# Router logits of a mixture-of-experts layer: the turned tokens as stationary operand, the router's 8 columns streaming

## The reference

```python
xf = x.reshape(-1, d)
gate_base = xf @ Wg.T
up_base = xf @ Wu.T
base_out = jax.nn.silu(gate_base) * up_base @ Wd.T
router_logits = xf @ Wr.T            # Wr is 8 x 256
probs = jax.nn.softmax(router_logits.astype(jnp.float32), axis=-1)
topw, topi = jax.lax.top_k(probs, K) # K = 2 of E = 8
...
def expert_step(acc, params):
    g_lora = xf @ Ag_e.T @ Bg_e.T * SCALING
    u_lora = xf @ Au_e.T @ Bu_e.T * SCALING
    h = jax.nn.silu(gate_base + g_lora) * (up_base + u_lora)
    d_delta = h @ Ad_e.T @ Bd_e.T * SCALING
    return (acc + d_delta * we[:, None], None)
```

## Time and profile before

| | |
|---|---|
| runs | 847.05, 847.84, 850.38 us, median 847.84 |
| the profiled execution's own time | 848.89 us |
| its span, first to last instruction | 847.2 us |
| TensorE busy | 737.8 us, 87% of the span, 4038 matmuls |
| VectorE, ScalarE, GpSimd busy | 524.9, 376.5 and 147.1 us |
| mean granted TensorE clock | 0.937 of full speed |

### The profile page before, as it was taken

One profiled execution on the slowest core, in us unless ns is written; L12 is line 12 of the kernel. 1 busy time (PEld: TensorE's weight loads), 2 busy tenths in 40 slices (PEclk: granted clock), 3 DMA queues, 4 the chain that ended last, 5 costly groups with the idle time before them and its releaser, 6 DMA issues. The chain is left out here.

```text
span 847.2 us, 10572 instructions
## 1 busy us (share of the span) xinstructions
PE 737.8 (87%) x4038; PEld 612.6 (72%) x4038; DVE 524.9 (62%) x927; ACT 376.5 (44%) x780; POOL 147.1 (17%) x115
## 2 busy tenths in 40 slices
PE   2798978775999999999999999999487999999956
PEld 1577767664787777887688777887265887878846
DVE  5545554654577545755475645755447888979883
ACT  4765545514465432544344433344255355254421
POOL 5065354331000001000010000000020223203110
PEclk9979999865999999999999999999689999999978
DMA  4075333100000000000000000040000000000000
GB/s 161 0 231 170 102 66 107 55 1 0 1 1 1 1 2 0 1 1 1 1 1 1 1 0 1 3 197 2 0 1 0 1 26 1 1 26 1 26 0 26
DMA packets 21282, 25.75 MB, mean 30 GB/s; under 512 B 976, under 2 KB 19408, under 8 KB 20464
## 3 DMA queue, kind: packets, MB, share of 16 engines
q1 hardware_dynamic: 20576, 23.76, 8.7%
q10 hardware_dynamic: 656, 1.31, 0.4%
HBM read 22.91 MB, written 2.16 MB: 30 GB/s over the span
## 5 line engine op out<-in xcount | busy, mean ns | idle before, releaser
L1014 DVE TENSOR_TENSOR h_raw<-h_s,bank 128x512 f32<-128x512 f32 x104 | 71.4, 687 | 148.3 <-ACT h_s L1004 129.6
L1004 ACT ACTIVATE h_s<-bank 128x512 f32<-128x512 f32 x104 | 62.1, 597 | 185.3 <-PE bank L91 185.3
L1019 DVE TENSOR_TENSOR h_ring_lo<-h_raw,h_ring_hi 128x512 fp32r<-128x512 f32 x104 | 76.9, 739 | 0.1
L1008 ACT ACTIVATE h_ring_hi<-h_raw 128x512 fp32r<-128x512 f32 x104 | 64.7, 622 | 0.2 <-DVE h_raw L1014 0.2
L90 PE MATMUL bank<-fused_lo,h_ring_hi 128*128 128x256 f32 (+1 forms) x224 | 62.8, 280 | 0.0
L89 PE MATMUL bank<-l_xT_hi,l_wgu 128*128 128x512 f32 x128 | 52.5, 410 | 8.2 <-DVE l_h L1899 5.9
L89 PE MATMUL bank<-f_xT_hi,ffn_hi 128*128 128x512 f32 (+2 forms) x120 | 47.8, 399 | 7.6 <-DVE f_xT_lo L1421 7.1
L1368 POOL TENSOR_TENSOR late_rstd<-f_vv,minus_half 128x4 f32<-128x4 f32 x4 | 4.0, 1009 | 289.1 <-DVE f_vv L1512 289.1
L89 PE MATMUL bank<-f_yT_hi,mlp_hi 128*128 128x512 f32 x128 | 52.4, 409 | 1.6 <-issue 1.6
L91 PE MATMUL bank<-l_xT_hi,l_lo 128*128 128x512 f32 x128 | 50.8, 397 | 0.0
L90 PE MATMUL bank<-l_xT_lo,l_wgu 128*128 128x512 f32 x128 | 50.8, 397 | 0.0
(11 more groups left out here) (303 smaller groups left out, 2112.4 us busy)
## 6 DMA issues: line engine op xcount, KB each, us to landing
m_W<-m_scratch SPq DMA_DIRECT2D x16, 512.0 KB, 5.9
fused_raw<-in_fused SPq DMA_DIRECT2D x1, 3584.0 KB, 15.9
res<-in_x SPq DMA_DIRECT2D x4, 512.0 KB, 6.1
fused_raw<-in_fused SPq DMA_DIRECT2D x2, 1024.0 KB, 8.3
l_raw<-in_layer SPq DMA_DIRECT2D x1, 2048.0 KB, 10.0
out_x<-res SPq DMA_DIRECT2D x16, 128.0 KB, 1.9
l_raw<-in_layer SPq DMA_DIRECT2D x1, 1280.0 KB, 12.4
fused_raw<-in_fused SPq DMA_DIRECT2D x1, 1120.0 KB, 5.1
```

The lines of the kernel that those rows point to most:

```text
L1004: self.nc.scalar.activation(self.s[u % 2][r, :], gate[r, :], ACT.Silu).then_inc(self.silu.sem, 1)
L1008: self.nc.scalar.activation(self.unit(i, u)[0], self.product(i, u), ACT.Copy).then_inc(self.hi.sem, 1)
L1014: self.nc.vector.tensor_tensor(out=self.product(i, u), in0=self.s[u % 2][r, :], in1=up[r, :], op=ALU.mult).then_inc(self.hidden.sem, 1)
L1019: self.nc.vector.tensor_tensor(out=lo, in0=self.product(i, u), in1=f32(hi), op=ALU.subtract).then_inc(self.lo.sem, 1)
```

## The change

The logits are made the other way round. For each chunk of 128 tokens the turned tokens are the stationary operand (128 x 128) and the router's 8 real columns stream, so the result has its tokens in the partitions at once. VectorE reads that result directly; the copy on ScalarE and the four turns on TensorE go away, and with them the tile `f_lg` and two semaphores.

```diff
@@ router_and_ranks
-                for k in range(KD):
-                    last = product(nc, turn_bank[0][0:EW, :], cut(wr, a, k), cut(xT, a, k), k == 0, k == KD - 1)
+                for c in range(C):
+                    for k in range(KD):
+                        last = product(nc, turn_bank[0][:, c * E:(c + 1) * E], cut(xT, a, k, chunk(c)), cut(wr, a, k, slice(0, E)), c == 0 and k == 0, k == KD - 1)
                 last.then_inc(lg_ready.sem, 1)
                 ranks(i, 0)
...
-            def turn_router(i):
-                pe.wait_ge(lg_copied.sem, lg_copied.at(i, 1))
-                for c in range(C):
-                    last = nc.tensor.transpose(turn_bank[0][:, c * EW:(c + 1) * EW], lg[:, chunk(c)], ident[0:EW, 0:EW])
-                last.then_inc(lgT.sem, 1)
...
-                    elif u == 4:
-                        turn_router(i)
...
-            def copy_router(i):
-                act.wait_ge(lg_ready.sem, lg_ready.at(i, 1))
-                nc.scalar.activation(lg[:, :], turn_bank[0][0:EW, :], ACT.Copy).then_inc(lg_copied.sem, 1)
...
-                        copy_router(i)
                         high_ranks(i, 0)
...
-            lgv = turn_bank[0][:, 0:C * EW].rearrange("p (c e) -> p c e", e=EW)[:, :, 0:E]
+            lgv = turn_bank[0][:, 0:C * E].rearrange("p (c e) -> p c e", e=E)
...
-                dve.wait_ge(lgT.sem, lgT.at(i, 1))
+                dve.wait_ge(lg_ready.sem, lg_ready.at(i, 1))
```

More of the change, by code:

```diff
@@ L1081, in fused_phase @@
     xs, ys = over("f_xs", [P, C, D]), over("f_ys", [P, C, D])
-    lg = Map(nc, spread_at + 4 * C * D)("f_lg", [EW, S])
     op0 = [m.pair("f_op0", [P, S])]
@@ L1104, in fused_phase @@
     yT_t, yT_hi, yT_lo, xs_ready, xT_t, xT_hi, xT_lo = (sg("f_" + n, 2) for n in ("yTt", "yThi", "yTlo", "xs", "xTt", "xThi", "xTlo"))
-    lg_ready, lg_copied, lgT, centred, exped = (sg("f_" + n, 1) for n in ("lg", "lgc", "lgT", "cent", "exp"))
+    lg_ready, centred, exped = (sg("f_" + n, 1) for n in ("lg", "cent", "exp"))
     a_done, a_hi, a_lo = sg("f_a", 2), sg("f_ahi", 2), sg("f_alo", 2)
```

## The result

| | before | changed |
|---|---|---|
| median of the runs | 849.11 us (847.05 to 851.92, 4 runs) | 864.94 us (861.09 to 865.25, 4 runs) |
| profiled execution: own time, span | 848.89, 847.2 us | 861.09, 859.3 us |
| mean granted clock in it | 0.937 | 0.928 |

The ratio is 1.0174, 95% interval 1.013 to 1.0217: slower by 1.3 to 2.2%. On the median that the prediction worked from, 847.84 us, the ratio makes 862.6 us; the two medians themselves stand 15.8 us apart. The three executions of the changed kernel other than the profiled one took 864.76 to 865.25 us at a mean granted clock of 0.920 to 0.922, so the profiled one lost the least clock of the four.

What follows compares the result with a forecast made beforehand. TensorE was taken to bound the fused phase; plain work of +2.9 us and clock loss of +11.9 us made +14.8 us on a median of 847.84, so 862.6 us. The forecast's own range was 854 to 870 us, 8 in 10 850 to 869.

Steps and rivals of the forecast that it cites:

- TensorE is the bound of the phase: Fused phase: TensorE busy 375.98 of 385.80 us, so work added or removed there reaches the end one for one.
- The copy is worth nothing: ScalarE's copy of the logits, 586 ns a turn, first read about 10 us later; removing it gains nothing.
- The six products and the turns: TensorE work removed from each fused-phase turn: six router products, 1.40 us, and four turns of the logits, 0.56 us.
- The 24 products at 0.112 us: New router products on TensorE, 8 columns streamed and 128 stationary loaded: 0.112 us each, 2.69 us a turn.
- Plain work +0.73 us a turn: TensorE's router work: 2.69 added less 1.40 and 0.56 removed, +0.73 us a turn, +2.9 us in four.
- The clock falls in every turn: Behind each router, pause and narrow products leave TensorE's array nearly idle, so its clock drops to 1.2 GHz; +11.9 us.
- seven stretches: Half-clock stretches of some 3.4 us, 1.7 us lost in each: two in three turns, one in the fourth; 11.9 us.
- The reason given for two stretches: The pause precedes the narrow products, so the clock's fall mostly finds them running, at half speed too; 3.4 us lost.
- The time of 862.6 us: Forecast median of the changed kernel: 847.84 us plus 14.8 us.
- one thing of 4.6 us: TensorE's 1.95 us pause plus 24 narrow products within 2.7 us, taken as one stretch of almost no array work.
- Mean clock -0.015: Sign to look for in the profile: the mean granted clock falls from 0.937 by some 0.015.
- rival 4: Behind the routers the clock falls in only one or two turns, one stretch each; 847 to 854 us, chance 0.08.

Runs made afterwards that it cites:

- the spread kernel: Changed kernel with its 24 router products of 8 columns a turn in four groups of six between dense products; 1.0086 of the kernel before.
- those with the pause filled: Kernel before and spread variant, each with unit 4's gate and up products moved ahead of the wait for `f_xT_lo`; 0.9912 and 0.9947 of the unmoved kernel before.
- the one with the ranks first: Changed kernel with the six `ranks` products of 512 columns put between the pause and the unbroken row of 24 router products; 1.0102 of the kernel before.
- the one with 256 columns: Changed kernel with each of the 24 router products streaming 256 weight columns instead of 8, same loads; 1.0043 of the kernel before.
- the kernel with the pause filled: Changed kernel with unit 4's gate and up products moved ahead of the wait for `f_xT_lo`, the narrow row in one piece; 0.9976 of the kernel before.
- the one without the turns: Kernel before without the four turns of the logits on TensorE, so the chosen experts are not the reference's; 0.9991 of the kernel before.
- the second profile: The changed kernel unaltered, timed and profiled again; 1.0145 of the kernel before, fused phase 415.36 us.

## Why the prediction was right

- **TensorE is the bound of the phase.** Shown: 12.16 of 12.2 us lie in it, the half-clock stretches are full of TensorE's work, ScalarE waits for it, and the turns of the logits, taken off TensorE alone, shortened a turn by the 0.6 us that they had cost.
- **The copy is worth nothing.** Nothing in the waits of TensorE answers to it, but no run leaves out the copy alone, so this is argued.
- **The six products and the turns.** 1.40 us was read off; the turns were put at 0.56 us and measured 0.6.
- **The 24 products at 0.112 us.** Measured 0.111 from 8 to 128 columns. The nearest row was the right one: as many stationary columns, another width. At 1.2 GHz the distance was 0.213 us. By the Trainium skill's load cost ("TensorE: Matmul & The Clock Gate", "LDWEIGHTS (loading the stationary operand)") it would be 107 ns, an estimate: the trace agrees within 5 ns at 2.4 GHz. It does not agree for the turns of the logits, which load 128 columns too and follow each other at 0.07 us. The floor of 25 ns for narrow products in the Trainium skill's "Back-to-back issue gap", same page, was not what bound here: 8 columns took 0.111 us.
- **Plain work +0.73 us a turn.** 0.6 to 0.7 in the turns of the changed kernel with their clock loss taken off, 0.8 in clean turns of the spread kernel, 0.6 in those with the pause filled. Why the last two differ is open.
- **The clock falls in every turn.** Shown in two profiles. Wider streams with the same loads took it away but for one turn; the same narrow products, spread and with the pause filled, kept the clock at 1.00 throughout. The loss, 11.9 us by seven stretches, was six stretches (10.2 us) in the first profile and eight (13.6 us) in the second. The reason given for two stretches, that the fall would find narrow products running, also held: it found them running in every turn that had two or three.
- **The time of 862.6 us.** That the ratio makes the very same figure is luck. The profiled execution grew by 12.2 us and the medians by 15.8 where 14.8 was forecast, and seven stretches were a choice between bounds of four and twelve. The range and the mechanism are what the prediction had right.
- **What was too simple.** I wrote of pause and narrow row as one thing of 4.6 us. They are two: the pause alone brought the clock down in turn 2 of the spread kernel, of the one with the ranks first and, by its place in time, of the one with 256 columns, and the row alone did in one turn of the kernel with the pause filled. Side by side, with 8, 32 or 128 columns, they brought it down in all 16 turns. The pause with dense products behind it held in all eight turns of the kernel before and the one without the turns, so one profile with the clock at 1.00 does not show that it always holds; whether the kernel before ever loses it there, no profile shows.
- **Mean clock -0.015.** It fell by 0.009 in one profile and 0.021 in the other. The other phases share in this mean: the second profile comes to the fused phase 4.9 us later (211.01 against 206.16).
- **Slips that change nothing.** TensorE's strip is full from the eleventh slice on, not the tenth. By its own terms rival 4 starts at 848.4 us, not 847, and the forecast's range ends at 871, not 870. The second short stretch of the earlier trace rows was also busy for more than half, 1.69 of 3.30 us.

What stays open: how the chip weighs streaming against time. That columns thinner in time are worth less is shown for one arrangement, 128 columns behind the pause. Each arrangement has one profile of four turns, the changed kernel two, so how often a lone pause or a lone row brings the clock down is known only roughly. Where in the row the clock falls differed between executions of the same kernel, and nothing here says why.

## What to carry to other kernels

A product with few streaming columns costs its weight load, here 0.111 us for 128 stationary columns whether 8 or 128 stream; so compare counts of loads, not columns, before turning operands round. Where TensorE is the bound, look at what stands next to its longest pauses: a row of narrow products beside a pause can cost several times in clock what it adds in plain work (here 10.2 and 13.6 us in two profiles against some 2.8), and a busy strip does not show it. The pause itself was the better target: 12 dense products a turn moved into it gave 7.7 us.

## What was not expected of the hardware

The mLSTM phase is the same code in all these kernels, and yet the first gate product behind it started at 205.30 us in one profile and at 211.01 in another; the clock falls in that phase at different places. From 40 us to the rise of the clock just behind that product the half-clock stretches add up to 61 us in the first and 82 us in the second. The difference in the start is 5.7 us, 0.7%, with no change in the work, and of the size by which the times of one kernel lie apart: 847.01 to 855.40 us for the kernel before, one stray execution of 1799.46 us left out. Differences below some 4 us are better read in this kernel from distances within a profile than from its times.
